# A residual block with two 3x3 convolutions: x's outer planes by a negation and an adding DMA two steps ahead, and the inner planes of conv 2 split one by one

## The reference

```
out = relu(bn1(conv3x3(x, w1)))          # stride 1, padding 1
out = bn2(conv3x3(out, w2))
return relu(out + x)
bn(x) = x * inv + (beta - mean * inv),  inv = gamma * rsqrt(var + 1e-5)
```

## Time and profile before

| | busy | share of the span |
|---|---|---|
| TensorE (PE) | 570.0 us | 93% |
| weight loads (PEld) | 553.2 us | 91% |
| VectorE (DVE) | 549.7 us | 90% |
| ScalarE (ACT) | 487.7 us | 80% |
| GpSimd (POOL) | 47.9 us | 8% |

### The profile page before, as it was taken

The page is one execution under the profiler, slowest core; times in us unless marked ns, Lnnn a source line. Parts: engine busy times, 40 slices in busy tenths (PEclk is TensorE's granted clock), DMA queues, the critical chain, the costliest instruction groups (busy, mean ns, idle before and its releaser), DMA issues.

```text
span 610.5 us, 8987 instructions
## 1 busy us (share of the span) xinstructions
PE 570.0 (93%) x3090; PEld 553.2 (91%) x3090; DVE 549.7 (90%) x443; ACT 487.7 (80%) x730; POOL 47.9 (8%) x52
## 2 busy tenths in 40 slices
PE   6769999999999999999999999999999999999997
PEld 3669999999999999999999999999999999999997
DVE  4699999999999999999999999999999999999974
ACT  4687789887788887787987778888778888778785
POOL 6700000000000000000000000000000000000000
PEclk9789999999999999999999999999999999999999
DMA  8444455435445444445443445534444534440112
GB/s 296 104 85 135 140 159 156 136 95 149 138 135 161 138 114 125 135 135 162 143 135 98 139 141 152 156 130 102 149 135 135 162 135 127 117 137 27 53 54 105
DMA packets 31679, 79.90 MB, mean 131 GB/s; under 512 B 2608, under 2 KB 19120, under 8 KB 31664
## 3 DMA queue, kind: packets, MB, share of 16 engines
q1 hardware_dynamic: 26912, 66.11, 29.9%
q0 software_dynamic: 4608, 13.31, 14.2%
q10 hardware_dynamic: 144, 0.29, 0.2%
HBM read 54.01 MB, written 25.69 MB: 131 GB/s over the span
## 4 chain that ended last, share of the span: by engine, by line
PE 56%; DVE 15%; issue 12%; ACT 12%; DMA 1%; POOL 0%; DVEq 0%; ACTq 0%
PE psum L669 56%; DVE ti_lo L449 9%; ACT out_sb L591 4%; DVE t_inner L433 3%; ACT hidden L568 3%; ACT z L563 2%; ACT z L562 2%; DVE t_inner L427 1%; ACT ti_hi L553 1%; DMA x_inner<-x_dram 1%; DVE psum L418 1%; ACT x_hi L533 0%; POOL w_mat L218 0%; DVE x_lo L404 0%; ACTq L560 0%
## 5 line engine op out<-in xcount | busy, mean ns | idle before, releaser
L669 PE MATMUL psum<-x_hi,w_hi 128*128 128x392 f32 (+2 forms) x512 | 176.3, 344 | 9.2 <-DVE x_lo L404 9.2
L669 PE MATMUL psum<-x_hi,w_lo 128*128 128x392 f32 (+2 forms) x512 | 175.5, 343 | 0.0
L669 PE MATMUL psum<-x_lo,w_hi 128*128 128x392 f32 (+2 forms) x512 | 175.3, 342 | 0.0
L418 DVE TENSOR_TENSOR psum<-psum,z 128x784 f32<-128x784 f32 (+1 forms) x128 | 127.1, 993 | 40.8 <-ACT hidden L568 14.4
L669 PE MATMUL psum<-ti_hi,w_hi 128*128 128x392 f32 x256 | 90.6, 354 | 23.8 <-DVE ti_lo L449 23.8
L669 PEld LDWEIGHTS psum<-x_hi,w_hi 128*128 128x128 f32 x512 | 97.4, 190 | 10.5 <-issue 6.3
L669 PEld LDWEIGHTS psum<-x_lo,w_hi 128*128 128x128 f32 x512 | 97.2, 190 | 0.4
L669 PEld LDWEIGHTS psum<-x_hi,w_lo 128*128 128x128 f32 x512 | 97.2, 190 | 0.4
L553 ACT ACTIVATE ti_hi<-t_inner 128x1624 fp32r<-128x1624 f32 (+2 forms) x33 | 50.3, 1524 | 54.2 <-DVE t_inner L433 54.2
L669 PE MATMUL psum<-h_hi,w_hi 128*128 128x392 f32 x256 | 87.2, 341 | 0.0
L669 PE MATMUL psum<-h_lo,w_hi 128*128 128x392 f32 x256 | 87.2, 341 | 0.0
(11 more groups left out here) (66 smaller groups left out, 829.3 us busy)
## 6 DMA issues: line engine op xcount, KB each, us to landing
x_sb<-x_dram SPq DMA_DIRECT2D x32, 814.0 KB, 4.8
out_dram<-out_sb SPq DMA_DIRECT2D x64, 392.0 KB, 2.8
x_inner<-x_dram SPq DMA_DIRECT2D x32, 406.0 KB, 3.2
x_inner<-x_dram POOLq DMA_DIRECT2D x32, 406.0 KB, 5.1
z<-w_dram ACTq DMA_DIRECT2D x1, 288.0 KB, 3.8
out_sb<-w_dram SPq DMA_DIRECT2D x1, 288.0 KB, 6.2
bn<-params_dram SPq DMA_DIRECT2D x1, 132.0 KB, 3.6
```

The source lines that it names most:

```text
L418: nc.vector.tensor_tensor(psum[:, half, EVEN:ODD + 1, 0:width], t1, z[:, half, :, 0:width], ALU.add).then_inc(joined[conv], 1)
L669: ins = nc.tensor.matmul(psum[:, half, bank, first:first + (j1 - j0) * WQ], w[:, i, far, :], moving, start=not onto and at == 0, stop=at = ...
```

## The change

It does four things.

1. The outer planes of x are no longer one VectorE subtraction. `negate_x` writes minus the second operand into `x_outer` (a tensor_scalar times -1), and GpSimd adds the first operand from memory with a second accumulating DMA (`add_outer`, 256 runs of 3248 bytes, twice the bytes of the inner one). `x_outer` gets two buffers.
2. `difference_x` and `negate_x` are made two steps ahead (image s+2 in step s); those of image 0 stand before VectorE's batch-norm arithmetic. The load of x_sb goes with them: image s+4 in step s, once image s+2 is negated, ahead of the stores in SP's order. The inner adding DMA now also waits for the difference.
3. `sum_hidden` moves ahead of `join(2, s-2, 1)`, and the inner planes of conv 2 are handled one by one: ScalarE rounds plane 1 ("t1") as soon as the sum is there, then does `relu_out(s-2, 0)`, then rounds plane 2 ("t2"); VectorE splits t1 before `join(1, s, 0)` and t2 after it. `outer_hidden` moves behind the split of t2.
4. On ScalarE `residual(s-1, 0)` moves ahead of `copy_sum(1, s, 1)`.

```diff
-        x_outer = sb("x_outer", [P, 2, RUN])
+        x_outer = sb("x_outer", [P, 2, 2, RUN])
...
             def step(s, k):
-                if not isinstance(s, int) or 0 <= s < N - 2:
-
-                    wait(sp, tx_ready["outer"], s + 3 - XBUFS)
-                    load(sp, s + 2, k + 2)
+                if not isinstance(s, int) or s + 4 < N:
+
+                    wait(sp, negated, s + 3)
+                    load(sp, s + 4, k + 4)
                 if there_is(s, s - 2):
                     store(s - 2, 0)
                     store(s - 2, 1)
...
-            def add_odd(n, k):
+            def add_inner(n, k):
 
                 pool.wait_ge(even_in[k], (n - k) * (16 // TBUFS) + 16)
+                pool.wait_ge(subtracted, n + 1)
                 odd = x_rows[n][:, XPLANE + 1:XPLANE + 1 + RUN]
-                pool.dma_start(x_inner[:, k, 0], odd, accum_op=ALU.add).then_inc(summed[k], 16)
+                pool.dma_start(x_inner[:, k, 0], odd, accum_op=ALU.add).then_inc(tx_ready["inner"][k % 2], 16)
+
+            def add_outer(n, k):
+
+                pool.wait_ge(negated, n + 1)
+                pool.dma_start(x_outer[:, k % 2], runs(x_rows[n], 0, XPLANE),
+                               accum_op=ALU.add).then_inc(tx_ready["outer"][k % 2], 16)
...
+            def negate_x(n, k):
+
+                wait(dve, xlo_ready["outer"], n - 1)
+                nc.vector.tensor_scalar(x_outer[:, k % 2], runs(x_sb[:, k % XBUFS], 1, XPLANE), -1.0, None,
+                                        ALU.mult).then_inc(negated, 1)
+
+            difference_x(0, 0)
+            negate_x(0, 0)
...
-            def outer_x(n, k):
-
-                wait(dve, xlo_ready["outer"], n)
-                cells = x_sb[:, k % XBUFS]
-                nc.vector.tensor_tensor(x_outer[:], runs(cells, 0, XPLANE), runs(cells, 1, XPLANE),
-                                        ALU.subtract).then_inc(tx_ready["outer"], 1)
...
+                if last:
+                    sum_hidden(s - 1)
                 if there_is(s, s - 2):
                     join(2, s - 2, 1, before_conv2(s - 2))
                 if last:
-                    sum_hidden(s - 1)
                     difference_hidden(s - 1)
-                    outer_hidden(s - 1)
+                    split_hidden("t1", s - 1, kl % 2)
                 if now:
                     join(1, s, 0, (2, s - 2))
-
-                if last:
-                    split_hidden("inner", s - 1, kl % 2)
-                if ahead:
-                    difference_x(s + 1, ka)
+                if last:
+                    split_hidden("t2", s - 1, kl % 2)
+                    outer_hidden(s - 1)
+                if there_is(s, s + 2):
+                    difference_x(s + 2, (k + 2) % 4)
                 if now:
                     join(1, s, 1, (2, s - 2))
 
-                if ahead:
-                    outer_x(s + 1, ka)
+                if there_is(s, s + 2):
+                    negate_x(s + 2, (k + 2) % 4)
...
                 if now:
                     copy_sum(1, s, 0)
                 if last:
-                    high_hidden("inner", s - 1, kl % 2)
+                    high_hidden("t1", s - 1, kl % 2)
                 if there_is(s, s - 2):
                     relu_out(s - 2, 0)
+                if last:
+                    high_hidden("t2", s - 1, kl % 2)
+                    residual(s - 1, kl, 0)
                 if now:
                     copy_sum(1, s, 1)
-                if last:
-                    residual(s - 1, kl, 0)
```

More of the change, by code:

```diff
@@ L115, in residual_block @@
             {which: sem(f"{what}_{which}") for which in sets} for what in ("filled", "mat", "whi", "wlo"))
+        subtracted, negated = sem("subtracted"), sem("negated")
         even_in = [sem(f"even_in{i}") for i in range(TBUFS)]
-        summed = [sem(f"summed{i}") for i in range(TBUFS)]
-        tx_ready = {"inner": sem("tx_inner"), "outer": sem("tx_outer")}
+        tx_ready = {which: [sem(f"tx_{which}{i}") for i in range(2)] for which in ("inner", "outer")}
         xhi_ready = {"inner": sem("xhi_inner"), "outer": sem("xhi_outer")}
         xlo_ready = {"inner": sem("xlo_inner"), "outer": sem("xlo_outer")}
-        th_ready = {"inner": sem("th_inner"), "outer": sem("th_outer")}
-        hhi_ready = {"inner": sem("hhi_inner"), "outer": sem("hhi_outer")}
-        hlo_ready = {"inner": sem("hlo_inner"), "outer": sem("hlo_outer")}
+        th_ready, hhi_ready, hlo_ready = (
+            {which: sem(f"{what}_{which}") for which in ("t1", "t2", "outer")} for what in ("th", "hhi", "hlo"))
         inner = {1: sem("inner1"), 2: sem("inner2")}
@@ L246, in x_full @@
         def x_full(which, k):
-            full, places = (x_outer[:], slice(0, 2)) if which == "outer" else (x_inner[:, k], slice(2, 4))
+            full, places = (x_outer[:, k % 2], slice(0, 2)) if which == "outer" else (x_inner[:, k], slice(2, 4))
             return full.rearrange("p s (j c) -> p s j c", c=WQ + 1)[:, :, :, 0:WQ], places
@@ L264, in hidden_parts @@
             rows = hidden_rows(half)
-            if which == "inner":
-                return t_inner[:, :, rows], ti_hi[:, :, rows], ti_lo[:, :, rows]
+            if which != "outer":
+                i = ("t1", "t2").index(which)
+                return t_inner[:, i, rows], ti_hi[:, i, rows], ti_lo[:, i, rows]
             return t_outer[:, :, rows], h_hi[:, b, :, rows], h_lo[:, b, :, rows]
@@ L368, in _, with difference_x @@
             fill_matrix(nc.vector.tensor_copy, "inner1", X_BLOCKS)
+            def difference_x(n, k):
+                dve.wait_ge(x_in[k % XBUFS], until(n, k))
+                wait(dve, res_ready, 2 * (n - TBUFS) + 2)
+                cells = runs(x_sb[:, k % XBUFS], 0, XPLANE + 1).rearrange("p s (j c) -> p s j c", c=WQ + 1)
+                nc.vector.tensor_tensor(x_full("inner", k)[0][:, 1], cells[:, 1, :, 0:WQ], cells[:, 0, :, 0:WQ],
+                                        ALU.subtract).then_inc(subtracted, 1)
+            def negate_x(n, k):
[4 more added lines that the diff above has]
+            negate_x(0, 0)
             after, part, row = chain(dve, bn_step[1]), slice(0, 2 + C), slice(2, 2 + C)
@@ L458, in step @@
                     outer_hidden(N - 1, 0)
-                    split_hidden("inner", N - 1, kl % 2, 0)
+                    split_hidden("t1", N - 1, kl % 2, 0)
+                    split_hidden("t2", N - 1, kl % 2, 0)
                     sum_hidden(N - 1, 1)
@@ L464, in step @@
                     outer_hidden(N - 1, 1)
-                    split_hidden("inner", N - 1, kl % 2, 1)
+                    split_hidden("t1", N - 1, kl % 2, 1)
+                    split_hidden("t2", N - 1, kl % 2, 1)
                     join(2, N - 1, 0, before_conv2(N - 1))
@@ L527, in high_x @@
                 full, places = x_full(which, k)
-                if which == "inner":
-                    act.wait_ge(summed[k], (n - k) * (16 // TBUFS) + 16)
-                act.wait_ge(tx_ready[which], n + 1)
+                act.wait_ge(tx_ready[which][k % 2], until(n, k))
                 wait(act, outer[1], 2 * (n - 1))
@@ L550, in high_hidden @@
                 act.wait_ge(th_ready[which], n + 1 + (half or 0))
-                wait(act, *((inner[2], 4 * n) if which == "inner" else (outer[2], 2 * (n - 1))))
+                wait(act, *((inner[2], 4 * n) if which != "outer" else (outer[2], 2 * (n - 1))))
                 nc.scalar.activation(hi, full, ACT.Copy).then_inc(hhi_ready[which], 1)
@@ L599, in step @@
                     residual(N - 1, kl, 0)
-                    high_hidden("inner", N - 1, kl % 2, 0)
+                    high_hidden("t1", N - 1, kl % 2, 0)
+                    high_hidden("t2", N - 1, kl % 2, 0)
                     relu_hidden(N - 1, 1)
@@ L604, in step @@
                     copy_sum(2, N - 1, 0)
-                    high_hidden("inner", N - 1, kl % 2, 1)
+                    high_hidden("t1", N - 1, kl % 2, 1)
+                    high_hidden("t2", N - 1, kl % 2, 1)
                     residual(N - 1, kl, 1)
@@ L686, in inner_products_2 @@
             def inner_products_2(n, half, more=0):
-                pe.wait_ge(hlo_ready["inner"], n + 1 + more)
+                pe.wait_ge(hlo_ready["t1"], n + 1 + more)
+                pe.wait_ge(hlo_ready["t2"], n + 1 + more)
                 pe.wait_ge(res_ready, 2 * n + half + 1)
```

21 lines of the change are left out of this document (10 added, 11 removed).

## The result

The kernel after takes 660.32 us (median of 4 runs, 660.16 to 660.75), the one before 612.39 in the same comparison: a ratio of 1.078 (95% interval 1.076 to 1.080), 48 us slower. The forecast was 588, the range 581 to 614. The profiled execution took 660.16 us, its span is 658.3. One of the four runs of experiment 4 took 929.15 us at a granted clock of 0.56, where every other run here had 0.97 or more, and is left out of that experiment's median.

What follows compares the result with a forecast made beforehand. TensorE was taken to bound the kernel, with one stall in each of thirty steps (18.105 to 17.11 us): 612.13 - 30 + 5.5 for the start = 587.6, forecast 588 us as median, range 581 to 614.

Steps and rivals of the forecast that it cites:

- DMAs: Added DMA traffic and later stores in each step: stores land 2.8 us after issue, with 9.4 us left before relu_out.
- rival B: Stores queued behind negation, load and outer add hold relu_out of half 0: 18.8 us a step, 639 us; chance 0.19.
- The stall: TensorE's wait in each step for conv 2's inner low parts and the residual: 1.04 us, expected to go.
- the floor: TensorE's time for one of the thirty equal steps without its waits: 17.07 us.
- the tight loops: Loops on ScalarE and VectorE over one step, both just under 17.07 us; 0.04 us allowed for them.
- loop (a): ScalarE from relu_out half 1 through x_hi inner, then x_lo inner and conv 2's join: P+16.98, P being the step's first matmul.
- The start: Before the equal steps: two earlier VectorE instructions and outer planes arriving by DMA delay conv 2's first product, +5.5 us.
- Rival A: The tight loops cost 0.3 to 0.8 us more a step through semaphores or traffic: 17.6 us, 603 us; chance 0.23.

Runs made afterwards that it cites:

- experiment 4: The kernel before with only the new order of conv 2's inner planes and of the residual, x's planes and DMAs as before: 589.09 us, repeated at 589.43 us.
- experiment 1: The kernel after with SP's two stores issued ahead of the wait for the negation and the x_sb load: 593.46 us, ratio to before 0.968.
- experiment 3: The kernel after with two output buffers, so relu_out waits for the store before last, DMAs and their order unchanged: 591.67 us, ratio to before 0.965.
- experiment 8: The kernel after with stores first and the outer planes of images 0 and 1 subtracted, without their adding DMAs: 586.86 us, ratio to before 0.958.
- experiment 2: The kernel after with outer planes made by VectorE's subtraction and no outer adding DMA, SP's order kept: 591.07 us, ratio to before 0.964.
- experiment 7: The kernel after with one outer plane subtracted and the other negated and added in 128 packets: 621.30 us, ratio to before 1.015.

## Why the prediction was wrong

**The step that failed** is the one in *DMAs*: "They take 2.8 us now, and 9.4 are left." It set the store's landing of an undisturbed queue against the slack. The change had just moved the store behind the negation, into the same microseconds as both adds and the load, so the landing to use was that of a store among them: 11.6 us. The mechanism stood in the text as rival B, with the place as measured and the deciding point (a landing over 9.4 us) near the 9.1 that the runs give, and was given 0.19 because of the earlier trace rows: between 10 and 11 us the plain queue had been served alone. That window says which queue went first once; it does not say how two queues with ready packets share the engines. After the change one step holds both: the load served alone, then the stores in turns with the outer add. The better reading was the one that stood beside it: stores and add wait for the same instruction, and nothing in the rows put the stores ahead.

**B's own size.** It gave 18.8 us a step, measured 19.73 to 19.80. (Its sum has 0.7 for what its text puts at 0.6; by the text it is 18.5 before the allowance for gaps.) Of the missing 0.9, 0.43 is the store's issue (R+8.13 for R+7.7) and 0.5 the landing. The inner add is issued later and longer, and its packets flow from R+8.0 and not R+6.7:

```profile
305.51 1.28 POOL L333 DMA_DIRECT2D x_inner<-x_dram  x1 [16.53 <-DVE x_inner L386]
307.31 1.20 POOL L338 DMA_DIRECT2D x_outer<-x_dram  x1 [0.52 <-issue]
```

So the 21 us that B gave its steps (30 of 0.7) became 44 (26 of 1.70), and 639 became 660.

**The step was mis-sized.** The stall was taken as 1.04 us a step from the idle time of the weight loads, the floor as 17.07, and 0.04 was added for the tight loops: 17.11. Experiments 1, 3 and 8 give 17.22. TensorE in the kernel before, around the stall:

```profile
293.96 0.34 PE L669 MATMUL psum<-h_lo,w_hi 128*128 128x392 f32 x1
295.02 0.45 PE L669 MATMUL psum<-ti_hi,w_hi 128*128 128x392 f32 x1 [0.72 <-DVE ti_lo L449]
295.30 0.34 PE L669 MATMUL psum<-ti_hi,w_lo 128*128 128x392 f32 x1
```

At a pitch of 0.18 the second was due at 294.14 and came 0.88 late; the third was due at 294.32 and came 0.98 late, and from there on the pitch is 0.18 again. So TensorE loses 0.98, and its floor is 18.105 - 0.98 = 17.13. The other 0.09 of the 17.22 is a new, small loss, in the inner products of conv 2 for half 1 (0.09 on the mean in experiments 1, 3 and 8, here from experiment 8):

```profile
288.15 0.34 PE L700 MATMUL psum<-x_lo,w_hi 128*128 128x392 f32 x1
288.35 0.41 PE L700 MATMUL psum<-ti_hi,w_hi 128*128 128x392 f32 x1
288.61 0.34 PE L700 MATMUL psum<-ti_hi,w_lo 128*128 128x392 f32 x1
```

ScalarE's residual of that half ends at 288.21 (287.27 + 0.94), just before; that TensorE waits for it is likely, but the trace names no releaser. So the floor was 0.06 too low and the allowance of 0.04 measured 0.09; over thirty steps that is 3 us of the forecast. The recorded sum of loop (a) is off too: its terms (8.76 + 3.96 + 1.51 + 1.70 + 0.97) give P+16.90 and not P+16.98.

**The start** came out at +5.7 by the first relu_out of half 0 (forecast 5.5), with x_hi of the outer planes of image 0 at 22.84 (forecast 22), of image 1 at 38.35 (39), and the first inner product of conv 2 at 46.66 (47):

```profile
22.84 1.51 ACT L549 ACTIVATE x_hi<-x_outer 128x1568 fp32r<-128x1568 f32 x1 [4.13 <-DMA x_outer<-x_dram]
...
38.35 1.51 ACT L549 ACTIVATE x_hi<-x_outer 128x1568 fp32r<-128x1568 f32 x1 [2.14 <-DMA x_outer<-x_dram]
```

Experiment 1 issues the same instructions up to there, and its profile has that product at 48.68; its runs spread over 3.3 us (592.57 to 595.83). The start varies between executions, and with it what it costs: the second x_hi came at 40.36 there. By the first relu_out of half 0 it cost +9.0 in experiment 1 (64.75) and +5.1 in experiment 3 (60.82), so that 5.7 came so near to 5.5 is in part luck.

**Right** were: the split of the planes removes TensorE's stall (experiment 4); the negation at a pitch of 0.9 us (rows below: 1.00 as its duration, and the next instruction 0.91 after its start); relu_out of half 0 released by TensorE wherever the store is in time; no wait of TensorE for the parts that the later outer_hidden makes, in experiments 1, 4 and 8.

```profile
305.67 1.00 DVE L392 TENSOR_SCALAR x_outer<-x_sb 128x1624 f32<-128x1624 f32 x1
306.58 1.84 DVE L464 TENSOR_TENSOR h_lo<-t_outer,h_hi 128x1624 fp32r<-128x1624 f32 x1
```

The POOL queue's share was forecast as 43% for a step of 17.1 and measured as 38.5% over the span in experiment 1, 34.6% in the longer kernel after.

**Rival A** is not seen in the changed kernel beyond the 0.09 above, but in small where the subtraction stays. With the subtraction (experiments 2 and 4) the step is 17.36, with the negation (1, 3, 8) 17.22. The difference lies in the first matmuls of a step, which by the program wait for the join of conv 2; experiment 4:

```profile
309.79 0.33 PE L676 MATMUL psum<-x_lo,w_hi 128*128 128x364 f32 x1
310.02 0.43 PE L676 MATMUL psum<-x_hi,w_hi 128*128 128x420 f32 x1
310.29 0.35 PE L676 MATMUL psum<-x_hi,w_lo 128*128 128x420 f32 x1
```

The second and the third start 0.23 and 0.27 us after the one before, where the pitch is 0.18; that is the place of rival A, at 0.14 us a step for the 0.3 to 0.8 that it gave. So the negation, with 24.9 MB more in POOL's queue (38.25 for 13.31 in experiment 8), buys 3.9 us over 29 steps and costs, where images 0 and 1 are subtracted, 1.7 at the start (first relu_out of half 0 at 56.26, for 54.55 in the repeat of experiment 4 beside it). That leaves 2.2, as the two spans differ (587.6 and 585.4); the medians differ by 2.6.

## What to carry to other kernels

When a change moves a DMA behind a wait, price its landing in the company that it will have there, packet by packet against every queue active then, and compare that with the slack of whoever waits for its buffer; a landing from the old place says nothing. A single output buffer makes "relu to store issue plus landing" a period of its own, which no busy share shows. Take a stall of TensorE from the starts of its matmuls, up to where they run at their pitch again (0.88 us at the first late one, 0.98 at the next; the idle time of the weight loads said 1.04), and look for the wait that comes next once it is gone.

## What the hardware showed beside this

**VectorE and GpSimd exclude each other, and the first to start keeps going.** In the start the second image's outer planes meet GpSimd's w_lo. First the two instructions in the kernel after, then in experiment 2, then in experiment 4 (start, duration):

```profile
30.07 3.16 POOL L231 TENSOR_TENSOR w_lo<-w_mat,w_hi 128x1024 fp32r<-128x1024 f32 x1
```
```profile
30.45 3.65 DVE L392 TENSOR_SCALAR x_outer<-x_sb 128x1624 f32<-128x1624 f32 x1
```
```profile
27.59 2.40 POOL L231 TENSOR_TENSOR w_lo<-w_mat,w_hi 128x1024 fp32r<-128x1024 f32 x1 [0.79 <-ACT w_hi L224]
```
```profile
27.70 4.00 DVE L385 TENSOR_TENSOR x_outer<-x_sb 128x1624 f32<-128x1624 f32 x1
```
```profile
26.74 1.84 DVE L396 TENSOR_TENSOR x_outer<-x_sb 128x1624 f32<-128x1624 f32 x1
```
```profile
26.85 3.97 POOL L231 TENSOR_TENSOR w_lo<-w_mat,w_hi 128x1024 fp32r<-128x1024 f32 x1 [1.81 <-ACT w_hi L224]
```

In the first two GpSimd starts first, and VectorE's instruction ends 0.87 and 1.71 us after GpSimd's (34.10 for 33.23, 31.70 for 29.99), about its own duration alone. In the third VectorE is 0.11 us ahead, takes its usual 1.84, and GpSimd's is the long one (3.97 for 2.40). That is the rule of the Trainium skill (SBUF — State Buffer, Who interferes with whom), that whoever issues first holds the shared ports for the whole instruction; the trace agrees. GpSimd's 3.16 in the first case is longer than the 2.40 of the second although it started first; what held it there isn't shown.

**The issue of an accumulating DMA takes longer beside a negation**: 1268 ns on the mean for the inner add in the kernel after (32 issues), 877 in experiment 2 and 887 in experiment 4, where no tensor_scalar of 1624 elements runs near it, and 900 in experiment 7, where the negation has half the size and stands behind a subtraction:

```profile
L333 POOL DMA_DIRECT2D x_inner<-x_dram x32 | 40.6, 1268 | 486.0 <-DVE x_inner L386 486.0
```
```profile
L333 POOL DMA_DIRECT2D x_inner<-x_dram x32 | 28.0, 877 | 480.2 <-DVE x_inner L378 480.2
```

That fits the same exclusion, but no run changed only what runs beside the issue, so it isn't shown to be the cause.

**Two queues share the engines in both ways within a step**: one for one (313 to 318) and one after the other (the inner add, then the load). The load's issue came at 306.87, 0.5 us before the add's first packet (307.4), and its packets still went after. What picks the one or the other was not settled; after reading only the second, the forecast went wrong.
